# A two-layer cross-attention kernel: the layer norm between the layers done in two halves of its columns

## The reference

```python
# layer 0: 32 query heads of 16, 8 key/value heads
out = softmax(q @ k.T * scale + mask) @ v             # per head, put together to (100, 512)
out = out @ Wo + bo
x = out + hidden_state
mu, var = mean(x, -1), var(x, -1)
x = (x - mu) * rsqrt(var + 1e-6) * gamma + beta       # the layer norm of this case
# layer 1: 16 heads of 32 on the same context, normalised
Q = x @ Wq.T                                          # first thing that layer 1 does with x
...
return x + tanh(gate) * (softmax(Q K.T) V) @ Wo.T
```

## Time and profile before

| | |
|---|---|
| median of 3 timed runs | 1306.05 us (1305.42 to 1306.56) |
| profiled execution, its own time | 1300.32 us |
| its span from the first to the last instruction | 1298.5 us |
| PE busy | 1199.8 us, 92% of the span |
| PEld busy | 904.9 us, 70% |
| DVE busy | 788.1 us, 61% |
| ACT busy | 746.2 us, 57% |
| POOL busy | 262.4 us, 20% |
| mean granted TensorE clock | 0.979 of full speed |

### The profile page before, as it was taken

The page is one execution under the profiler, slowest core; times in us unless marked ns, Lnnn a source line. Parts: engine busy times, 40 slices in busy tenths (PEclk is TensorE's granted clock), DMA queues, the critical chain, the costliest instruction groups (busy, mean ns, idle before and its releaser), DMA issues.

```text
span 1298.5 us, 31567 instructions
## 1 busy us (share of the span) xinstructions
PE 1199.8 (92%) x9768; PEld 904.9 (70%) x9768; DVE 788.1 (61%) x2321; ACT 746.2 (57%) x2147; POOL 262.4 (20%) x280
## 2 busy tenths in 40 slices
PE   4899999989999998999999899999989999898977
PEld 4666776767777776777777677777767777676755
DVE  3365657656575765656666575766757476665634
ACT  3274647647474674747567474756747475574733
POOL 2221213121121212112131211312121131211210
PEclk9799999999999999999999999999999999999986
DMA  7663626346362634736264473526437353653500
GB/s 238 169 168 86 163 71 155 92 107 169 77 170 61 153 104 96 179 77 161 59 155 112 95 180 76 151 70 138 130 84 191 67 156 76 129 138 84 141 1 7
DMA packets 77820, 153.75 MB, mean 118 GB/s; under 512 B 10384, under 2 KB 47056, under 8 KB 77152
## 3 DMA queue, kind: packets, MB, share of 16 engines
q1 hardware_dynamic: 77792, 153.40, 48.7%
HBM read 113.72 MB, written 39.65 MB: 118 GB/s over the span
## 4 chain that ended last, share of the span: by engine, by line
PE 73%; issue 10%; DVE 7%; ACT 5%; DMA 2%; POOL 1%; DVEq 1%; ACTq 0%; SPq 0%; POOLq 0%
PE PJ L354 18%; PE TP L405 13%; PE SCO L391 7%; PE OA L425 5%; PE SCO L628 5%; PE PJ L455 5%; PE PJ L367 4%; PE SCO L447 4%; PE SCO L395 3%; ACT PR L968 3%; DVE SCO L756 2%; PE SCO L354 1%; POOL YRS L1174 1%; PE OA L430 1%; DVE Y L907 1%
## 5 line engine op out<-in xcount | busy, mean ns | idle before, releaser
L968 ACT ACTIVATE PR<-SCO,MN 100x361 f32<-100x361 f32 x768 | 425.4, 564 | 209.1 <-DVE MN L756 209.0
L756 DVE CUSTOM_DVE_ANT_0 SCO<-SCO,MK 100x361 f32<-100x361 f32 x768 | 397.6, 551 | 171.2 <-PE SCO L391 137.8
L405 PE MATMUL TP<-ident,PR 100*128 100x100 f32 x2304 | 269.3, 253 | 8.5 <-ACT PT L981 6.1
L405 PEld LDWEIGHTS TP<-ident,PR 100*128 100x128 f32 x2304 | 234.0, 142 | 59.3 <-issue 12.8
L981 ACT ACTIVATE PT<-TP 121x600 f32<-121x600 f32 x256 | 172.3, 673 | 50.6 <-PE TP L405 50.3
L968 ACT ACTIVATION_READ_ACCUMULATOR PR<-SCO,MN 100x1 f32 x768 | 156.6, 204 | 0.0
L768 DVE COPY PT<-TP 121x600 f32<-121x600 f32 x128 | 100.1, 782 | 75.0 <-PE TP L405 73.6
L391 PE MATMUL SCO<-K0S,Q0S 64*100 64x362 f32 x512 | 127.9, 406 | 7.4 <-ACT PR L968 6.3
L395 PE MATMUL SCO<-K1S,Q1S 128*100 128x362 f32 x256 | 94.2, 403 | 28.0 <-ACT PR L968 23.7
L756 DVE DVE_READ_ACCUMULATOR2_ANT MN<- 100x1 f32 x768 | 108.1, 141 | 0.0
L354 PE MATMUL PJ<-TH,WK1h 128*128 128x364 f32 x256 | 92.5, 361 | 0.3 <-DVE K1F L748 0.3
(11 more groups left out here) (138 smaller groups left out, 1793.8 us busy)
## 6 DMA issues: line engine op xcount, KB each, us to landing
K1S<-k_scr SPq DMA_DIRECT2D x128, 364.0 KB, 6.1
k_scr<-K1HL SPq DMA_DIRECT2D x64, 364.0 KB, 2.6
Q0S<-q_scr SPq DMA_DIRECT2D x128, 100.0 KB, 4.0
K0S<-k_scr SPq DMA_DIRECT2D x64, 182.0 KB, 5.3
AT<-ctx_cols SPq DMA_DIRECT2D x16, 722.0 KB, 9.3
V<-ctx_rows SPq DMA_DIRECT2D x16, 484.0 KB
q_scr<-QHL SPq DMA_DIRECT2D x16, 400.0 KB, 2.5
k_scr<-KHL SPq DMA_DIRECT2D x32, 182.0 KB, 3.0
```

The costliest lines, as they stand in the source:

```text
L405: last = pe.transpose(TP[:, k % 2, c * T:(c + 1) * T], PR[0:T, k % NPR, c * SP:c * SP + P], ident[0:T, 0:T])
L756: dve.tensor_tensor_reduce(out=bank, in0=bank, in1=mask[0:T, :], scale=scale, scalar=3.4e38, op0=ALU.add, op1=ALU.min, accum_out=MN[0:T, k ...
L968: act.activation(PR[0:T, k % NPR, 0:S], SCO[0:T, k % 3, 0:S], ACT.Exp, bias=MN[0:T, k:k + 1], scale=-1.0, accum_out=SM[0:T, k:k + 1]).then ...
```

## The change

The seam is cut into two halves of 256 columns. `out0` becomes eight matmuls of 256 columns: the first four go to bank 2 of `SCO`, the other four to bank 0, and each group raises `out0_mm`. DVE adds and takes `bn_stats` of one half, then of the other; `YST` holds two sets of statistics, which `bn_aggr` joins. L903 and L907 become two instructions each, and each half of `Y` raises `y_ok`. PE transposes the first two 128-column blocks of `Y` into bank 0 after the first `y_ok`, and the other two into bank 2 after the second. ACT copies them in two pieces of 200 columns, each with its own `yt_mm` and `yt_ev`. The query projection starts after the first `yt_ev` and waits for the second ahead of its third matmul. Nothing moves to another engine, and the filling work keeps its place.

```diff
--- before.py
+++ after.py
@@ -106,7 +106,7 @@
         OT = sb("OT", [P, C, T])
 
         R0, Y = sb("R0", [P, D]), sb("Y", [P, D])
-        YST, YMV, YVE, YRS = sb("YST", [P, 6]), sb("YMV", [P, 2]), sb("YVE", [P, 1]), sb("YRS", [P, 1])
+        YST, YMV, YVE, YRS = sb("YST", [P, 2, 6]), sb("YMV", [P, 2]), sb("YVE", [P, 1]), sb("YRS", [P, 1])
         YT = OT
         WK1_raw = PT_flat[:, 0:C * D].rearrange("p (c n) -> p c n", c=C)
         WV1_raw = PT_flat[:, WV1_AT:WV1_AT + C * D].rearrange("p (c n) -> p c n", c=C)
@@ -443,9 +443,11 @@
                 last.then_inc(sums_t, 1)
 
             def out0(b):
-                for c in range(C):
-                    last = pe.matmul(SCO[0:T, 2, :], OT[:, c, :], WO0[:, c, :], start=c == 0, stop=c == C - 1)
-                last.then_inc(out0_mm, 1)
+                for half in range(2):
+                    cols = slice(half * (D // 2), (half + 1) * (D // 2))
+                    for c in range(C):
+                        last = pe.matmul(SCO[0:T, 2 - 2 * half, cols], OT[:, c, :], WO0[:, c, cols], start=c == 0, stop=c == C - 1)
+                    last.then_inc(out0_mm, 1)
 
             def out1(b, steps):
 
@@ -613,18 +615,22 @@
                     keys0(range(6, 12))
                     pe.wait_ge(q0_l, 4 * b + 8)
                     values0()
-                pe.wait_ge(y_ok, b + 1)
                 for c in range(C):
-                    last = pe.transpose(SCO[:, 0, c * T:(c + 1) * T], Y[0:T, c * P:(c + 1) * P], ident[0:T, 0:T])
-                last.then_inc(yt_mm, 1)
+                    if c % 2 == 0:
+                        pe.wait_ge(y_ok, 2 * b + c // 2 + 1)
+                    last = pe.transpose(SCO[:, c // 2 * 2, c * T:(c + 1) * T], Y[0:T, c * P:(c + 1) * P], ident[0:T, 0:T])
+                    if c % 2 == 1:
+                        last.then_inc(yt_mm, 1)
                 if more:
                     pe.wait_ge(v1_ev, 3 * b + 3)
                     for i in range(3):
                         keys1(b + 1, i)
                     pe.wait_ge(k0_l, b + 2)
-                pe.wait_ge(yt_ev, b + 1)
+                pe.wait_ge(yt_ev, 2 * b + 1)
                 for m in range(C):
                     for c in range(C):
+                        if m == 0 and c == 2:
+                            pe.wait_ge(yt_ev, 2 * b + 2)
                         last = pe.matmul(SCO[:, 1, m * T:(m + 1) * T], WQ1[:, c, m * P:(m + 1) * P], YT[:, c, :],
                                          start=c == 0, stop=c == C - 1)
                 last.then_inc(q1_mm, 1)
@@ -889,23 +895,29 @@
                 if more:
                     queries0_low(b + 1)
 
-                dve.wait_ge(out0_mm, b + 1)
                 dve.wait_ge(xb, b + 1)
-                dve.tensor_tensor(R0[0:T, :], SCO[0:T, 2, :], R0[0:T, :], ALU.add).then_inc(res, 1)
-                dve.wait_ge(res, b + 1)
-                dve.bn_stats(YST[0:T, :], R0[0:T, :]).then_inc(y_st, 1)
-                dve.wait_ge(y_st, b + 1)
+                for half in range(2):
+                    cols = slice(half * (D // 2), (half + 1) * (D // 2))
+                    dve.wait_ge(out0_mm, 2 * b + half + 1)
+                    dve.tensor_tensor(R0[0:T, cols], SCO[0:T, 2 - 2 * half, cols], R0[0:T, cols], ALU.add).then_inc(res, 1)
+                    dve.wait_ge(res, 2 * b + half + 1)
+                    dve.bn_stats(YST[0:T, half, :], R0[0:T, cols]).then_inc(y_st, 1)
+                dve.wait_ge(y_st, 2 * b + 2)
                 dve.sem_inc(met_dve, 1)
-                dve.bn_aggr(YMV[0:T, :], YST[0:T, :]).then_inc(y_mv, 1)
+                dve.bn_aggr(YMV[0:T, :], YST[0:T, :, :]).then_inc(y_mv, 1)
                 dve.wait_ge(y_mv, b + 1)
                 dve.sem_inc(met_dve, 1)
                 dve.tensor_scalar(YVE[0:T, :], YMV[0:T, 1:2], EPS0, None, ALU.add).then_inc(y_ve, 1)
-                dve.scalar_tensor_tensor(out=Y[0:T, :], in0=R0[0:T, :], scalar=YMV[0:T, 0:1], in1=G0[0:T, :],
-                                         op0=ALU.subtract, op1=ALU.mult).then_inc(y_n, 1)
-                dve.wait_ge(y_n, b + 1)
+                for half in range(2):
+                    cols = slice(half * (D // 2), (half + 1) * (D // 2))
+                    dve.scalar_tensor_tensor(out=Y[0:T, cols], in0=R0[0:T, cols], scalar=YMV[0:T, 0:1],
+                                             in1=G0[0:T, cols], op0=ALU.subtract, op1=ALU.mult).then_inc(y_n, 1)
                 dve.wait_ge(y_rs, b + 1)
-                dve.scalar_tensor_tensor(out=Y[0:T, :], in0=Y[0:T, :], scalar=YRS[0:T, 0:1], in1=B0[0:T, :],
-                                         op0=ALU.mult, op1=ALU.add).then_inc(y_ok, 1)
+                for half in range(2):
+                    cols = slice(half * (D // 2), (half + 1) * (D // 2))
+                    dve.wait_ge(y_n, 2 * b + half + 1)
+                    dve.scalar_tensor_tensor(out=Y[0:T, cols], in0=Y[0:T, cols], scalar=YRS[0:T, 0:1],
+                                             in1=B0[0:T, cols], op0=ALU.mult, op1=ALU.add).then_inc(y_ok, 1)
                 if more:
                     keys0_low(b + 1)
                 dve.wait_ge(q1_h, b + 1)
@@ -1071,9 +1083,10 @@
                 unit_sums(b, 1, 2 * T)
                 if more:
                     keys0_high(b + 1)
-                act.wait_ge(yt_mm, b + 1)
-                act.activation(YT[:, :, :].rearrange("p c t -> p (c t)"), SCO[:, 0, 0:C * T], ACT.Copy)\
-                    .then_inc(yt_ev, 1)
+                for half in range(2):
+                    act.wait_ge(yt_mm, 2 * b + half + 1)
+                    act.activation(YT[:, 2 * half:2 * half + 2, :].rearrange("p c t -> p (c t)"),
+                                   SCO[:, 2 * half, 2 * half * T:2 * half * T + 2 * T], ACT.Copy).then_inc(yt_ev, 1)
                 if more:
                     values0_copied(b + 1)
                 act.wait_ge(q1_mm, b + 1)
@@ -1176,7 +1189,7 @@
                     rstd_diagonal(b + 1)
                     keys1_low(b + 1, 0)
                     keys1_low(b + 1, 1)
-                pool.wait_ge(yt_mm, b + 1)
+                pool.wait_ge(yt_mm, 2 * b + 2)
                 pool.wait_ge(gb_ev, 1)
                 pool.tensor_tensor(Y[0:T, :], Y[0:T, :], GB[0:T, :], ALU.add).then_inc(y_b, 1)
 
```

## The result

| | before | changed |
|---|---|---|
| median of four timed runs each, us | 1305.74 (1303.02 to 1306.56) | 1281.42 (1279.38 to 1282.30) |
| ratio | | 0.9821 (0.9805 to 0.9836) |
| profiled execution, its own time / span, us | 1300.32 / 1298.5 | 1280.66 / 1278.9 |
| PE busy, us / share | 1199.8 / 92% | 1198.4 / 94% |
| from one output projection to the next (median of 13), us | 76.25 | 74.97 |

PE does the same amount of work, and stands still less.

A forecast was written before the change was run, and what follows sets the result against it. PE was taken to set the time (73% of the chain), idling at the seam. 15 x 0.66 + 1.0 = 10.9 us off 1306.05 gave 1295.1 us, with 1290.0 to 1301.0 to hold 8 in 10.

The forecast's parts named there:

- The output projection: `out0` as sixteen records of 256 columns instead of eight of 512 takes 3.79 us, 0.11 more, on the path.
- Sum and statistics: First half on DVE hidden under `out0`, second half's two instructions 2 x 0.265 us shorter: L899 starts 0.42 earlier.
- The first scaling and the power on POOL: L903 in halves holds POOL until the second half ends: 0.13 us lost, so the rstd comes 0.29 earlier.
- rival 1: POOL gets in between the halves of L903: gain 0.85 to 1.06 us per batch, about 1290.5 us; chance 0.12.
- The start of the second scaling: L907, behind POOL's power, starts 0.29 us earlier, at 646.36 instead of 646.65.
- The second scaling, transposes and copies: Last `y_ok` 0.16 us earlier, two transposes fewer behind it 0.17, ACT's copy hidden 0.32: 0.66 per batch.
- What follows the projection moves with it: Everything behind the query projection's start was taken to move rigidly with it.
- The last batch: Without filling work, the query projection starts at about 1255.6 against 1256.64: 1.0 us gained, nothing counted for the clock.
- Rival 2: The added waits break PE's flow: gain 0.32 us per batch, 5.5 in all, 1300.5 us; chance 0.15.
- Rivals 3 and 4: 3: halves on DVE and ACT aren't cheap, 1320.8 us, chance 0.06; 4: gain given back behind the seam, 1306, chance 0.07.

## Why the prediction was wrong

The direction and the mechanism stood: PE idles at the seam for DVE and ACT, and the halves shorten what it waits for. The size was off: 0.66 a batch instead of 1.27. By the prediction's own steps:

- **The output projection: mis-sized.** 0.11 more was forecast, 0.02 was measured (3.70 against 3.68). I took the spacing of 256-column matmuls, 0.227, from eight records of `out1`; sixteen of `out0` start (3.70 - 0.38) / 15 = 0.221 apart. In both only the first gap is long, 0.30, and the others are 0.216, so an average over seven can't be stretched over fifteen. And what counts is the signal of the last, at 3.73 as against 3.71. 0.09 too pessimistic.
- **Sum and statistics: right.** 0.42 and 0.43 measured, 0.42 forecast. The joined `bn_aggr` cost 0.03 (0.21 against 0.18), which I had put at nothing.
- **The first scaling and the power on POOL: this is the step that failed.** I saw that POOL is held back by L903 and had both ends, +0.13 and -0.27, and chose the first "since the halves leave no gap between them". The runs show the hand-over after the first half: 0.73 in all sixteen batches of the changed kernel and in fifteen with the halved scaling alone, 0.99 with it whole, 0.55 with one SBUF operand. In the changed kernel the power is 0.26 shorter, so this term alone is 0.39 a batch, 6 us in all. The overlap by which I argued is of one instruction's start with the other's end and didn't keep POOL out. The Trainium skill ("SBUF — State Buffer", Who interferes with whom) has the shared port kept for the length of one instruction, in words that it writes of DVE's two-port modes; the runs agree for two SBUF operands, with 0.73 and 0.99, and by that rule my own rival 1 was the better choice.
- **The start of the second scaling: a term that I had carried over without a reason.** I let it come 0.12 after the power's end as before; it came 0.03 after, 0.09 more. In the changed kernel the wait for the power rides on the scaling, in the kernel before it is an instruction of its own; the listings in the section on the change have the two waits in opposite orders, and I booked nothing for it. By the traces that is the cause; an edit that changes it alone was not run.
- **The second scaling, transposes and copies: right.** 0.88 for the two scalings, the projection 0.81 after the last `y_ok` (0.80 forecast), ACT's copy hidden, and worth the 0.32.
- **What follows the projection moves with it: right, and 0.08 better,** since the projection's first weights load while PE still works.
- **The last batch: 1.0 forecast, 1.4 measured** (means of four executions each). PE's pause ahead of the transposes fell from 4.1 to 3.0 us and the clock fell all the same: the query projection took 5.45 to 7.06 us there, 6.24 to 7.07 before.

0.09 + 0.39 + 0.09 + 0.08 less 0.03 for the aggregation and 0.01 for rounding is the missing 0.61. In the whole program the fifteen seams gave 18.9 us where 9.9 were forecast: 9 of the 13.7 us by which the total missed. Rival 1 gave 0.85 to 1.06 a batch and about 1290.5 us; it was the right mechanism with the other terms too small. Rival 2 (added waits) fell: the changed projection is shorter than the old one, with its second wait in it, and the 0.2 us of idle before the second pair of transposes is DVE's time. Rivals 3 and 4 fell with the durations of 0.42 to 0.48 and the period. The Trainium skill's advice ("VectorE: DVE Perf Modes", The TRN2 errata) against tiles under 512 elements does not hold here: DVE is busy for 11.1 us more (799.2 against 788.1), and the kernel is faster all the same, since PE doesn't wait for the added part.

The total adds two things that I hadn't looked at. I held the distance between the profiled and the timed runs for a constant (5.7 us); it was the luck of one profile. And the last batch depends on the clock by 3 us either way, which one profile can't show.

## What to carry to other kernels

Where PE waits at the end of a short chain through two or three engines, cutting the chain by columns pays twice: the first half hides under the producer, and each hand-over is as long as a half. A small GpSimd operation beside a long VectorE instruction with two SBUF operands should be costed from that instruction's end; shorten or split the VectorE instruction, or feed one operand from PSUM, before making the GpSimd operation itself cheaper. Of an instruction's waits, look at which one the sequencer takes as an instruction of its own: if it is the one that ends last, the work behind it starts later, here by 0.07 to 0.10 us. And when the ends of a program vary with the clock, compare the period of its loop: it repeated to 0.02 us, while the total wavered by 3 either way.

## What the runs showed of the hardware that I had not expected

- A one-column power on POOL: 0.55 us beside a DVE instruction with one SBUF operand, 0.73 beside two halves and 0.99 beside one whole with two. It ends 0.41 us after the DVE instruction in flight, and gets in between two that overlap by 0.08.
- DVE is not delayed by that: the two halves took 0.87 us with POOL between them, and 0.86 reading PSUM, with POOL free.
- 32 records of a matmul behind a wait took 3.79 us, and 3.71 where the wait was already fulfilled.
- A DVE instruction started 0.03 us after the POOL instruction that it waited for where the wait rode on it, 0.11 after where a separate semaphore instruction waited, and 0.13 where a register instruction did. This is read from ten kernels that differ in more than that.
